# The last mixing chunk sent from SBUF to SBUF into the tokens, and tile 0's statistics moved ahead of the tables

## The chip, the cores and the metric

The kernel runs on one core of a Trainium2 chip. The metric is the device time of one execution in microseconds. Its median was 815.43 us in 3 runs (813.94 to 815.71).

## The reference, cut to what matters

The kernel computes one layer of a token-mixing tower. A state-space kernel of length 512 for 256 channels is generated from the input `x` (8, 256, 64, 2); its result is the token tensor `h` of 8 batches, 256 tokens (the channels of the mixing) and 512 features. To it come a windowed attention with rotary embedding on the layer norm of `h` (16 query heads, 4 key and value heads, head size 128, window 256) and a gated low-rank feed-forward on the layer norm of the sum.

```python
    # mixing: H, N, L = 256, 64, 512
    dtA = w * dt[:, None]
    Cm = Cc * (jnp.exp(dtA) - 1.0) / w
    h = 2 * jnp.einsum('chn,hnl->chl', Cm, jnp.exp(dtA[:, :, None] * jnp.arange(L))).real
    ...
    h = h + _L0_attn_ref(_layernorm(h, axis=-1), w_q, w_k, w_v, w_o)
    h = h + _L0_ffn_ref(_layernorm(h, axis=-1), ...)
```

Both matter here only through this: the layer norm of batch 0 needs the tokens of all 16 mixing chunks.

## The kernel before

**Mixing.** The 256 tokens are worked on in NQ = 16 chunks `q`. A chunk holds 8 tokens of each of two halves `hh` (tokens `hh*128 + 8q` to `hh*128 + 8q + 7`). For a chunk GpSimd, DVE and ACT write factor tables, TensorE multiplies 128 small pieces (`chunk`, L1426) into two PSUM banks, one for each `hh`, and counts `mixed`. ACT evacuates both banks into the stage tile `st[s]` (`evacuate`, L726) and counts `evac`. In `st` the partitions are (token parity t, batch c, feature block a) and the free dimensions four token pairs `m` and 64 features `j`.

**Through DRAM.** SP stores `st` into the DRAM tensor `mixed` (`store_mixed`, L427, two transfers of 128 KB, semaphore `xd_out[s]`) and loads tokens back into `x` (`load_tokens`, L431, two transfers of 64 tokens of one batch). `x` has 128 partitions, two token tiles t of 128 tokens, 8 batches and 512 features. Token tile 0 is made of the chunks 0 to 7, tile 1 of the chunks 8 to 15; partition `hh*64 + i` of tile t is token `hh*128 + 64t + i`. SP's order is written out by hand: after chunk 7 the load of tile 0 of batch 0 (`x_early`), then one store and one load in turn, then the store of chunk 15, a wait for all stores, and the loads of tile 1: batch 0 (`x_first`), batch 1 (`x_second`), batch 2 (`x_third`), two loads of weights, and the other batches (`x_rest`).

**The first layer norm, in halves.** DVE, after its last mixing work (L1054), multiplies the tables of the feed-forward (L1082 to L1085, twelve products, semaphore `pw_done`). Then it takes the statistics of tile 0 of batch 0 (`norm_stat`, L1089, and the aggregate at L1155, `early_var`), waits for GpSimd's `early_rstd`, applies the norm (`half_apply(0)`, L1145, `early_xn`), subtracts the rounded part of the transposed tile (`half_rest(0)`, L1149), waits for `x_first`, and does the same for tile 1 (aggregate L1164, `ln_var`, `half_apply(1)`). GpSimd waits for `pw_done`, makes the low part of the first weight chunk (`split_lo(0)`, L480), the reciprocal root for tile 0 (`early_norm`, L387, L540, L542), the low parts of the chunks 1 to 3 and then the root for tile 1 (`second_norm`, L387, L552, L554). ACT, after its last evacuation, copies `cw` (L761), loads the table of exponentials (L762) and copies the transposed halves (`xt_half`, L765). TensorE, after the last chunk, multiplies the tables (`cw_mm`, L1463), keeps its clock up with matmuls on constants (`keep_warm`, L1440), transposes tile 0 (L1473), keeps warm again, transposes tile 1 (L1473), keeps warm once more and begins the first projection (`split_product`, L1414 to L1416) with 48 matmuls of 256 columns.

**Order.** Every engine works its program in order, and a wait holds up all that stands behind it on that engine. The lines that set the order around the change are SP's list (L437 to L450), GpSimd's (L536 to L547), ACT's (L756 to L765), DVE's (L1076 to L1166) and TensorE's (L1461 to L1478).

Of the kernel before, what the change touches and what calls it, by code (L numbers as in the profile page):

```python
# [22 lines left out]
ACT = mybir.ActivationFunctionType  # L23
# [6 lines left out]
NS = 64  # L30
# [102 lines left out]
def tower(nc, mix_c, mix_s, log_dt, log_wr, w_im, w_qkv, w_o, w_gate, w_gmul, w_upd, centers, slopes, consts, out):  # L133
    x_dram = nc.dram_tensor("mixed", [S, NB, D], F32, kind="Internal").ap()
    top = ExitStack()
    with top:
        def sem(name):
            return top.enter_context(nc.semaphore(name))
# [171 lines left out]
        def raw_turn(n):  # L310
# [18 lines left out]
            sem("early_var"), sem("early_pool"), sem("early_rstd"), sem("early_xn"), sem("early_xt"), sem("early_hi"),  # L329
            sem("early_lo"), sem("x_early"))  # L330
        pw_done, cw_mm, cw_done = sem("pw_done"), sem("cw_mm"), sem("cw_done")
        ln_st, ln_var, ln_pool, ln_rstd, xn_ready = (
# [19 lines left out]
        def half_rows(hh):  # L352

            return slice(hh * NS, (hh + 1) * NS)

        def tokens_of(hh, t):

            first = hh * P + t * NS
            return slice(first, first + NS)
# [33 lines left out]
        def _(sp):  # L393
# [30 lines left out]
            def store_mixed(q, s, evacuated):  # L424
                sp.wait_ge(evac, evacuated)
                for hh in range(2):
                    sp.dma_start(rows[q, hh], st[s][:, hh, :, :]).then_inc(xd_out[s], 16)  # L427

            def load_tokens(t, b, done):
                for hh in range(2):  # L430
                    sp.dma_start(x[half_rows(hh), t, b, :], x_dram[tokens_of(hh, t), b, :]).then_inc(done, 16)  # L431

# [6 lines left out]
            for b, done in ((1, x_second), (2, x_third), (3, x_rest), (4, x_rest), (5, x_rest), (6, x_rest), (7, x_rest)):  # L439
                q = NQ // 2 + b - 1  # L440
                store_mixed(q, q % 2, q + 1)
                load_tokens(0, b, done)
            store_mixed(NQ - 1, 1, NQ)
            for s in range(2):
                sp.wait_ge(xd_out[s], 16 * 2 * (NQ // 2))
            load_tokens(1, 0, x_first)
            load_tokens(1, 1, x_second)
            load_tokens(1, 2, x_third)
# [22 lines left out]
        def _(pool):  # L471
# [57 lines left out]
            for hh in range(2):  # L529
                if hh:  # L530
                    pool.wait_ge(pb_done, 2)
                with pool.Fori(hh * NQ // 4 or 1, (hh + 1) * NQ // 4) as it:
                    for s in range(2):
                        pool.wait_ge(mixed, it * 2 + (s - 1))
                        chunk(it * 2 + s, s)
            pool.wait_ge(pw_done, KC)  # L536
            def early_norm():
# [5 lines left out]

            split_lo(0)
            early_norm()
            for n in range(1, KC):
                split_lo(n)  # L547
# [109 lines left out]
        def _(act):  # L657
# [86 lines left out]
            for lo, hi in ((1, TURN_AT), (TURN_AT, NQ // 2 - 1)):  # L744
                if lo == TURN_AT:
                    turn_p(1)
                with act.Fori(lo, hi) as it:
                    for s in range(2):
# [6 lines left out]
                        evacuate(it * 2 + s, s)  # L755
            for s in range(2):  # L756
                act.wait_ge(mixed, NQ - 1 + s)
                act.wait_ge(xd_out[s], (NQ // 2 - 1) * 32)
                evacuate(NQ - 2 + s, s)
            act.wait_ge(cw_mm, 1)  # L760
# [161 lines left out]
        def _(dve):  # L922
# [139 lines left out]
            for lo, hi in ((1, TURN_AT), (TURN_AT, NQ // 2)):  # L1062
# [6 lines left out]
                with dve.Fori(lo, hi) as it:  # L1069
                    for s in range(2):  # L1070
# [3 lines left out]
                        sum_b(s, it * 2 + s)  # L1074

            dve.wait_ge(gate_in, 80)  # L1076
            for k in range(KC):
# [8 lines left out]
                                dbs[:, k, :].unsqueeze(2).to_broadcast([P, NE, HE]), ALU.mult).then_inc(pw_done, 1)  # L1086

            def norm_stat(src, t):
                v.bn_stats(stats[:, t, :], src(t)).then_inc(ln_st, 1)  # L1089

# [25 lines left out]
            def tokens(b):  # L1116
                return lambda t: x[:, t, b, :]
# [33 lines left out]

            dve.wait_ge(x_early, 32)
            norm_stat(tokens(0), 0)
            wait_apart(dve, ln_st, 1, 4)
            v.bn_aggr(norm_set(0)["mv"][:, 0, :], stats[:, 0, :]).then_inc(early_var, 1)  # L1155
            dve.wait_ge(early_rstd, 1)
            half_apply(0).then_inc(early_xn, 1)
            for q in range(2):
                dve.wait_ge(early_hi, q + 1)
                half_rest(q, 0, 5 + q).then_inc(early_lo, 1)  # L1160
            dve.wait_ge(x_first, 32)
            norm_stat(tokens(0), 1)
            wait_apart(dve, ln_st, 2, 4)
# [243 lines left out]
        def _(pe):  # L1407
# [57 lines left out]

            pe.wait_ge(evac, NQ)
            keep_warm(2)

# [327 lines left out]
```

## Time and profile before

| | before |
|---|---|
| median of 3 runs | 815.43 us (813.94 to 815.71) |
| the profiled execution | 815.9 us |
| its span, first to last instruction | 813.8 us |
| TensorE busy | 748.4 us (92%) |
| VectorE (DVE) busy | 571.2 us (70%) |
| ScalarE (ACT) busy | 456.3 us (56%) |
| GpSimd (POOL) busy | 447.3 us (55%) |
| mean granted clock of TensorE | 0.994 |

The profile is of one execution. PE is TensorE, PEld its weight loads, SPq and ACTq the issue of transfers on SyncE and ScalarE. L with a number is a line of the kernel. The granted clock is given as a share of 2.4 GHz. The end of matmuls is modelled. A row of a timeline may merge several instructions of one line; its count stands behind the x. What ended the idle time before an instruction is inferred from semaphores and stands in brackets.

### The profile page before, as it was taken

How to read it: one execution, taken by the hardware profiler on the slowest of the kernel's cores; microseconds unless marked ns; L12 is line 12 of the kernel's file. 1: busy time of each engine (PE TensorE's matmuls, PEld its weight loads, DVE VectorE, ACT ScalarE, POOL GpSimd, SP SyncE). 2: the span in 40 equal slices, each digit the busy share in tenths (PEclk: the TensorE clock that was granted, in tenths of full speed). 3: DMA queues.
4: the chain of work that ended last, by engine and by line, in shares of the span. 5: the costliest groups of instructions: out<-in, count | busy, mean ns of one | idle time of the engine just before them, and what ended most of it. 6: DMA issues, size and time to landing. Idle time of an engine off the chain costs nothing.

```text
span 813.8 us, 19725 instructions
## 1 busy us (share of the span) xinstructions
PE 748.4 (92%) x6968; PEld 679.0 (83%) x6968; DVE 571.2 (70%) x1603; ACT 456.3 (56%) x1252; POOL 447.3 (55%) x663
## 2 busy tenths in 40 slices
PE   0377788999999999999999999999999999999996
PEld 0166667899999999999999999999999998988873
DVE  7989868877765655565665566666655777778876
ACT  6734436565567566555575655555756645545432
POOL 1488847655545646444465654444747565565532
PEclk9999999999999999999999999999999999999999
DMA  9023741100010102000001020000100001110104
GB/s 213 0 55 86 173 130 27 39 1 0 0 41 1 53 1 79 0 0 0 0 14 40 10 69 0 0 0 0 30 24 2 1 2 27 26 26 0 27 8 96
DMA packets 32215, 26.47 MB, mean 33 GB/s; under 512 B 23134, under 2 KB 23518, under 8 KB 32166
## 3 DMA queue, kind: packets, MB, share of 16 engines
q1 hardware_dynamic: 32022, 25.77, 12.7%
q8 instruction: 28, 0.46, 0.2%
q14 instruction: 21, 0.17, 0.1%
q10 hardware_dynamic: 144, 0.07, 0.0%
HBM read 17.44 MB, written 8.39 MB: 32 GB/s over the span
## 4 chain that ended last, share of the span: by engine, by line
PE 77%; POOL 7%; DVE 7%; ACT 4%; issue 3%; DMA 1%; DVEq 0%; SPq 0%; POOLq 0%; ACTq 0%
PE bank_quad L1414 17%; PE bank_quad L1416 16%; PE bank_quad L1415 16%; PE bank_pair L1414 4%; PE bank_pair L1416 4%; PE bank_pair L1415 4%; POOL w_lo L480 2%; PE bank_quad L1426 2%; PE bank_quad L1529 2%; PE bank L1607 1%; PE bank_pair L1597 1%; PE bank L1611 1%; PE bank_pair L1607 1%; DVE bank_pair L1043 1%; POOL kq_lo L572 1%
## 5 line engine op out<-in xcount | busy, mean ns | idle before, releaser
L1414 PE MATMUL bank_quad<-xt_hi,w_hi 128*128 (+1 forms) x768 | 216.7, 282 | 1.7 <-POOL w_lo L480 0.8
L1416 PE MATMUL bank_quad<-xt_lo,w_hi 128*128 (+1 forms) x768 | 214.4, 279 | 0.0
L1415 PE MATMUL bank_quad<-xt_hi,w_lo 128*128 (+1 forms) x768 | 214.3, 279 | 0.0
L1130 DVE TENSOR_TENSOR kq<-bank_quad,cst 128x512 f32<-128x512 f32 (+1 forms) x96 | 57.8, 603 | 134.3 <-ACT swap L793 101.2
L567 POOL TENSOR_TENSOR swap<-swap,cst 128x512 f32<-128x512 f32 (+1 forms) x96 | 106.0, 1106 | 81.2 <-ACT swap L793 77.0
L1414 PEld LDWEIGHTS bank_quad<-xt_hi,w_hi 128*128 128x128 f32 x768 | 144.2, 188 | 3.4 <-POOL w_lo L480 1.5
L1416 PEld LDWEIGHTS bank_quad<-xt_lo,w_hi 128*128 128x128 f32 x768 | 144.2, 188 | 0.0
L1415 PEld LDWEIGHTS bank_quad<-xt_hi,w_lo 128*128 128x128 f32 x768 | 143.9, 187 | 0.0
L387 POOL TENSOR_TENSOR spare<-cst 1x1 f32<-1x1 f32 x86 | 17.8, 208 | 200.3 <-DVE rinv L1296 139.7
L838 ACT ACTIVATE sm<-sm,mx 128x128 f32<-128x128 f32 (+1 forms) x256 | 113.6, 445 | 20.6 <-DVE mx L1284 20.6
L792 ACT ACTIVATE swap<-bank_quad 64x512 f32<-64x512 f32 (+1 forms) x96 | 50.3, 524 | 118.0 <-PE bank_quad L1416 115.1
L605 POOL TENSOR_SCALAR sm<-sm,rinv 128x128 f32<-128x128 f32 (+1 forms) x256 | 104.4, 421 | 0.9
L850 ACT ACTIVATE ot_hi<-bank_quad 128x512 fp32r<-128x512 f32 x64 | 37.8, 597 | 110.2 <-PE bank_quad L1416 110.2
L1136 DVE TENSOR_TENSOR kq<-kq,swap 128x512 f32<-128x512 f32 (+1 forms) x96 | 94.9, 1012 | 4.7 <-POOL swap L567 4.7
L572 POOL TENSOR_TENSOR kq_lo<-kq,kq_hi 128x256 fp32r<-128x256 f32 x93 | 78.5, 869 | 19.9 <-ACT kq_hi L804 19.9
L1275 DVE TENSOR_TENSOR ot_lo<-bank_quad,ot_hi 128x512 fp32r<-128x512 f32 x64 | 43.4, 677 | 25.7 <-ACT ot_hi L850 25.6
L1414 PE MATMUL bank_quad<-wo_hi,ot_hi 128*128 128x512 f32 x132 | 54.5, 413 | 0.4 <-DVE ot_lo L1275 0.4
L1416 PE MATMUL bank_quad<-wo_lo,ot_hi 128*128 128x512 f32 x132 | 51.9, 394 | 0.0
L1415 PE MATMUL bank_quad<-wo_hi,ot_lo 128*128 128x512 f32 x132 | 51.8, 393 | 0.0
L793 ACT ACTIVATE swap<-bank_quad 64x512 f32<-64x512 f32 (+1 forms) x96 | 49.9, 520 | 1.1
L1416 PE MATMUL bank_pair<-wo_lo,ot_hi 128*128 128x512 f32 x124 | 48.4, 390 | 0.0
L1415 PE MATMUL bank_pair<-wo_hi,ot_lo 128*128 128x512 f32 x124 | 48.2, 389 | 0.0
(332 smaller groups left out, 1867.7 us busy)
## 6 DMA issues: line engine op xcount, KB each, us to landing
mixed<-st SPq DMA_DIRECT2D x32, 128.0 KB, 2.0
x<-mixed SPq DMA_DIRECT2D x32, 128.0 KB, 3.1
out<-x SPq DMA_DIRECT2D x32, 128.0 KB, 2.3
raw<-in_w_qkv SPq DMA_DIRECT2D x8, 384.0 KB, 3.7
raw<-in_w_o SPq DMA_DIRECT2D x10, 256.0 KB, 2.7
norm_mem<-in_w_qkv SPq DMA_DIRECT2D x6, 384.0 KB, 3.7
norm_mem<-in_w_o SPq DMA_DIRECT2D x6, 256.0 KB, 2.8
cim<-in_mix_s SPq DMA_DIRECT2D x4, 256.0 KB, 7.9
```

The lines of the kernel that those rows point to most:

```text
L567: nc.gpsimd.tensor_tensor(view(sw), view(sw), table(sinT), ALU.mult).then_inc(rot_sin, 1)
L572: nc.gpsimd.tensor_tensor(flat(kl), part(kq), flat(kh).bitcast(F32), ALU.subtract).then_inc(kq_lo, 1)
L605: last = nc.gpsimd.tensor_scalar(sm[:, j, cols], sm[:, j, cols], rinv[:, 2 * j + t:2 * j + t + 1], 1.0, ALU.mult, ALU.mult)
L792: nc.scalar.activation(view(sw)[0:64], src[64:128], ACT.Copy)
L793: last = nc.scalar.activation(view(sw)[64:128], src[0:64], ACT.Copy)
L838: last = nc.scalar.activation(sm[:, j, cols], sm[:, j, cols], ACT.Exp, scale=-1.0, bias=mx[:, n:n + 1], accum_out=rsum[:, n:n + 1])
L1130: v.tensor_tensor(view(kq), src, table(cosT), ALU.mult).then_inc(kq_cos, 1)
L1136: v.tensor_tensor(view(kq), view(kq), view(sw), ALU.add).then_inc(kq_rot, 1)
L1275: v.tensor_tensor(by_rows(otl, j), natural(banks[j]), by_rows(oth, j).bitcast(F32), ALU.subtract).then_inc(ot_lo, 1)
L1414: mmul(dst, lh, rh, start=start and k == 0, stop=False, skip_group_check=True)
L1415: mmul(dst, ll, rh, start=False, stop=False, skip_group_check=True)
L1416: last = mmul(dst, lh, rl, start=False, stop=stop and k == n - 1, skip_group_check=True)
```

## The change

Chunk 15 no longer goes through DRAM. Its two banks are evacuated by two engines, bank 2 (`hh` = 0) by ACT and bank 3 (`hh` = 1) by DVE, each with a semaphore of its own. `last_rows` then sends each of the four token pairs `m` of a half straight from `st[1]` to two partitions of `x`, all batches at once: four transfers for `hh` = 0 issued by SP and four for `hh` = 1 issued by ACT, all counted on `x_last`. The loads of tile 1 shrink from 64 to 56 tokens. On SP the four stand behind the loads of batch 0, on ACT ahead of the copy of `cw`. DVE's statistics and aggregate of tile 0 move ahead of the table products. GpSimd makes the root for tile 0 first and all four low parts behind it, after `early_xn`. TensorE waits for chunk 14's evacuation instead of chunk 15's and keeps warm once instead of twice.

```diff
+        last_evac, x_last = [sem(f"last_evacuated{k}") for k in range(2)], sem("x_last_rows")
...
+        def last_rows(engine, hh):
+
+            first = hh * NS + NS - QH8
+            engine.wait_ge(last_evac[hh], 1)
+            for m in range(QH8 // 2):
+                engine_of = nc.sync if hh == 0 else nc.scalar
+                engine_of.dma_start(x[first + 2 * m:first + 2 * m + 2, TT - 1, :, :], st[1][:, hh, m, :]).then_inc(x_last, 16)
...
             def load_tokens(t, b, done):
+                n = NS if t == 0 else NS - QH8
                 for hh in range(2):
-                    sp.dma_start(x[half_rows(hh), t, b, :], x_dram[tokens_of(hh, t), b, :]).then_inc(done, 16)
+                    at, tok = half_rows(hh).start, tokens_of(hh, t).start
+                    sp.dma_start(x[at:at + n, t, b, :], x_dram[tok:tok + n, b, :]).then_inc(done, 16)
...
-            store_mixed(NQ - 1, 1, NQ)
             for s in range(2):
-                sp.wait_ge(xd_out[s], 16 * 2 * (NQ // 2))
+                sp.wait_ge(xd_out[s], 16 * 2 * (NQ // 2 - s))
             load_tokens(1, 0, x_first)
+            last_rows(sp, 0)
             load_tokens(1, 1, x_second)
...
-            pool.wait_ge(pw_done, KC)
             def early_norm():
...
-            split_lo(0)
             early_norm()
-            for n in range(1, KC):
+            pool.wait_ge(early_xn, 1)
+            pool.wait_ge(pw_done, KC)
+            for n in range(KC):
                 split_lo(n)
...
-            for s in range(2):
-                act.wait_ge(mixed, NQ - 1 + s)
-                act.wait_ge(xd_out[s], (NQ // 2 - 1) * 32)
-                evacuate(NQ - 2 + s, s)
+            act.wait_ge(mixed, NQ - 1)
+            act.wait_ge(xd_out[0], (NQ // 2 - 1) * 32)
+            evacuate(NQ - 2, 0)
+            act.wait_ge(mixed, NQ)
+            act.wait_ge(xd_out[1], (NQ // 2 - 1) * 32)
+            nc.scalar.activation(st[1][:, 0, :, :].rearrange("p m j -> p (m j)"), banks[2][:, 0:4 * 64],
+                                 ACT.Copy).then_inc(last_evac[0], 1)
+            last_rows(act, 1)
...
+            dve.wait_ge(x_early, 32)
+            norm_stat(lambda t: x[:, t, 0, :], 0)
+            wait_apart(dve, ln_st, 1, 4)
+            v.bn_aggr(norm_set(0)["mv"][:, 0, :], stats[:, 0, :]).then_inc(early_var, 1)
+
             dve.wait_ge(gate_in, 80)
...
-            dve.wait_ge(x_early, 32)
-            norm_stat(tokens(0), 0)
-            wait_apart(dve, ln_st, 1, 4)
-            v.bn_aggr(norm_set(0)["mv"][:, 0, :], stats[:, 0, :]).then_inc(early_var, 1)
             dve.wait_ge(early_rstd, 1)
             half_apply(0).then_inc(early_xn, 1)
+            dve.wait_ge(mixed, NQ)
+            dve.wait_ge(xd_out[1], (NQ // 2 - 1) * 32)
+            v.tensor_copy(st[1][:, 1, :, :].rearrange("p m j -> p (m j)"), banks[3][:, 0:4 * 64]).then_inc(last_evac[1], 1)
             for q in range(2):
                 dve.wait_ge(early_hi, q + 1)
                 half_rest(q, 0, 5 + q).then_inc(early_lo, 1)
             dve.wait_ge(x_first, 32)
+            dve.wait_ge(x_last, 16 * 8)
             norm_stat(tokens(0), 1)
...
-            pe.wait_ge(evac, NQ)
-            keep_warm(2)
+            pe.wait_ge(evac, NQ - 1)
+            keep_warm(1)
```

## Rows read from the trace of the kernel before

**Rows 1.** The page, the chain that ended last, shares of the span by engine.

```profile
PE 77%; POOL 7%; DVE 7%; ACT 4%; issue 3%; DMA 1%; DVEq 0%; SPq 0%; POOLq 0%; ACTq 0%
```

**Rows 2.** The chain in order of time, 95 to 110: start us, us, what.

```profile
98.27 0.67 ACT st L726 x2
...
99.37 2.16 DMA mixed<-st
...
102.14 2.92 DMA x<-mixed
105.09 0.70 DVE stats L1089
...
107.25 0.56 DVE norm_mem L1145
```

**Rows 3.** Timeline of GpSimd: start us, us, engine, line, operation [idle before, releaser].

```profile
97.21 1.82 POOL L480 TENSOR_TENSOR w_lo<-raw,w_hi 128x768 fp32r<-128x768 f32 x1 [2.27 <-DVE vtab L1085]
...
100.05 1.80 POOL L480 TENSOR_TENSOR w_lo<-raw,w_hi 128x768 fp32r<-128x768 f32 x1
101.81 3.79 POOL L480 TENSOR_TENSOR w_lo<-raw_more,w_hi 128x768 fp32r<-128x768 f32 x2
106.13 0.18 POOL L387 TENSOR_TENSOR spare<-cst 1x1 f32<-1x1 f32 x1 [0.53 <-DVE norm L1164]
```

**Rows 4.** Timeline of DVE, 95 to 104.

```profile
95.65 0.22 DVE L1082 TENSOR_TENSOR vtab<-fw 128x64 f32<-128x64 f32 x1
...
97.03 0.71 DVE L1089 BATCH_NORM_STATS2 stats<-x 128x6 f32<-128x512 f32 x1
...
100.12 2.02 DVE L1145 TENSOR_SCALAR norm_mem<-x,norm 128x512 f32<-128x512 f32 x1 [2.12 <-POOL norm L542]
103.08 0.42 DVE L1149 TENSOR_TENSOR xt_lo<-bank_pair,xt_hi 128x256 fp32r<-128x256 f32 x1 [0.95 <-ACT xt_hi L765]
```

**Rows 5.** Timelines of SP's issues and of ACT, 95 to 101.

```profile
95.79 0.93 SPq L427 DMA_DIRECT2D mixed<-st  x2
96.76 1.20 SPq L431 DMA_DIRECT2D x<-mixed  x2
...
99.67 1.28 ACT L762 ACT_TABLE_LOAD   x1
```

**Rows 6.** Issues and chain at the start; windows (engines busy, PEclk, DMA share, GB/s).

```profile
0.74 0.72 SPq L394 DMA_DIRECT2D lg<-in_log_dt  x1
...
0.73 0.39 ACTq L665 DMA_DIRECT2D lg<-in_log_wr  x1
...
0.74 3.54 DMA lg<-in_log_dt
...
2.20:2.40 0.20, 0.00 (x0) 0.00 (x0) 0.00 (x0) 0.20 (x1) 0.00 (x0) 1.00 0.14 44
5.50:6.00 0.50, 0.00 (x0) 0.00 (x0) 0.47 (x2) 0.00 (x0) 0.00 (x0) 1.00 1.06 408
50.50:51.50 1.00, 0.06 (x5) 0.06 (x6) 1.00 (x2) 0.00 (x0) 0.94 (x1) 1.00 1.05 218
```

**Rows 7.** Timeline of TensorE, 99 to 108.

```profile
99.16 1.88 PE L1440 MATMUL bank_quad<-cst 128*128 128x512 f32 x4
102.19 0.44 PE L1473 MATMUL bank_pair<-cst,norm_mem 128*128 128x128 f32 x2 [1.15 <-DVE norm_mem L1145]
...
102.68 3.60 PE L1440 MATMUL bank_quad<-cst 128*128 128x512 f32 x8
107.94 0.41 PE L1473 MATMUL bank<-cst,norm_mem 128*128 128x128 f32 x2 [1.67 <-DVE norm_mem L1145]
```

**Rows 8.** TensorE after two idle stretches, and the window behind the second.

```profile
34.02 7.46 PE L1440 MATMUL bank_quad<-cst 128*128 128x512 f32 x10 [34.02 <-DVE vtab L1004]
...
66.11 0.38 PE L1435 MATMUL bank_quad<-bt,g 64*128 64x2 f32 x2 [2.92 <-DVE bt L1054]
...
66.00:72.00 6.00, 5.89 (x252) 5.75 (x256) 5.50 (x7) 2.04 (x8) 3.34 (x3) 0.72 0.17 35
```

More of the change, by code:

```diff
@@ L1074, in _, with norm_stat @@
                         sum_b(s, it * 2 + s)
+            def norm_stat(src, t):
+                v.bn_stats(stats[:, t, :], src(t)).then_inc(ln_st, 1)
+            dve.wait_ge(x_early, 32)
+            norm_stat(lambda t: x[:, t, 0, :], 0)
+            wait_apart(dve, ln_st, 1, 4)
+            v.bn_aggr(norm_set(0)["mv"][:, 0, :], stats[:, 0, :]).then_inc(early_var, 1)
             dve.wait_ge(gate_in, 80)
@@ L1086, in _ @@
                                 dbs[:, k, :].unsqueeze(2).to_broadcast([P, NE, HE]), ALU.mult).then_inc(pw_done, 1)
-            def norm_stat(src, t):
-                v.bn_stats(stats[:, t, :], src(t)).then_inc(ln_st, 1)
             def norm_collect(m):
```

## The prediction, made before the changed kernel ran

> **What bounds the kernel now.** I read three views in this order: the chain that ended last, then each engine's timeline around the hand-over from mixing to the layers, then the windows. Over the whole span the chain is mostly TensorE [rows 1], so from about 150 us on anything that starts TensorE later makes the end later by the same amount. The change touches only 95 to 110 us, where the chain is one transfer after another. Mixing's last chunk ends in ACT's evacuation at 98.27 us; SP issues its store in two halves, the second from 99.37, which lands in DRAM at 101.53 (99.37 + 2.16), the load back lands at 105.06 (102.14 + 2.92), and only then can DVE take tile 1's statistics at 105.09 [rows 2]. From 98.27 to 105.09 are 6.8 us, which is what the change aims at.
>
> Behind that chain stands a second one that is nearly as late. GpSimd splits four weight chunks (L480): it waits for the tables until 97.21, stops for tile 0's norm, and ends at 105.60 (101.81 + 3.79). It then waits 0.53 us for DVE's aggregate and starts tile 1's norm at 106.13, whose end releases `half_apply(1)` at 107.25 [rows 2, 3]. The time to be won is therefore not 6.8 us but what GpSimd leaves.
>
> **Tile 0's statistics ahead of the tables.** DVE's table products start at 95.65 [rows 4] and end at 97.03, where the statistics start [rows 4]. Exchanged, the statistics start at 95.65. For tile 1 it is 1.04 us from their start (105.09) to GpSimd's norm (106.13), and 1.12 us more to the apply (107.25) [rows 2, 3]. GpSimd is idle at this place (2.27 us before its first split [rows 3]), so it starts at 96.7 and `early_rstd` comes at 97.8. The tables end at 98.0. `half_apply(0)` then runs with GpSimd idle: 0.56 us as at 107.25 [rows 2], not 2.02 beside a running split [rows 4]. `early_xn` comes at about 98.6, 3.5 us before 102.14. GpSimd's four splits now wait for it and run without a stop: 98.63 + 1.80 for the first + 5.55 for the other three (100.05 to 105.60) = 105.98 [rows 3]. Tile 1's norm can thus start at 105.98, against 106.13. The greatest gain of the whole change is 0.15 us, whatever the transfers do.
>
> **The evacuation in two halves.** ACT copies bank 2 (98.27 to 98.65), DVE copies bank 3 after `half_apply(0)`. The copy of 256 columns from PSUM is bounded by 0.42 us, DVE's 256-column read of PSUM beside a running split [rows 4], and by 2.02 us if it had to wait as the apply did. I take 0.42, because the row of 0.42 also reads PSUM; DVE is done at 99.05.
>
> **The order of SP's queue.** The store of chunk 15 goes. SP is free at 97.96, after the loads that start at 96.76 [rows 5]. Chunk 14's store lands at about 98.35, since its second half is issued some 0.5 us behind 95.79 and takes the 2.1 us of a store [rows 2, 5]. The two loads for `x_first` are then issued from 98.4 to 99.6 (1.20 a pair [rows 5]), and behind them the four row transfers. The loads of the next batches come behind these. Issued at about 102.6 as they were before at 102.8, they cost nothing, as long as tile 1 is later than they are.
>
> **The eight row transfers: where the time goes.** Each writes 8192 floats into two partitions from 128 partitions, that is 128 pieces of 256 B. The trace has no SBUF-to-SBUF transfer. It has one that is two entries wide at its outermost level: the load of `log_dt`, whose source is two rows. Its issue took 0.72 us, ACT's ordinary one of the same bytes 0.39, and it landed 3.54 us after its issue; while it ran alone the DMA share was 0.14 at 44 GB/s, 2.2 of 16 engines at 20 GB/s each [rows 6]. A 512-B packet thus took 512 B / 20 GB/s, 25 ns. So a transfer with two entries outermost on one side ran on two engines, and the eight new ones have two partitions outermost on their destination side. I take two engines, and the same two for all eight, as SP's and ACT's transfers share the 16 engines.
>
> The Trainium skill, "DMA: Bandwidth & Descriptors", section "Why a DMA increments its semaphore by 16 and not by 1", says that the number of engines is the largest up to 16 that divides the slowest dimension of both sides, and that they are always the lowest-numbered ones. By that rule a two-partition destination gets two engines; for a source side the `log_dt` row agrees, for a destination side no row shows it.
>
> How long does a 256-B packet take an engine? Stores of such packets ran at 218 GB/s on all 16, 13.6 GB/s each: 256 / 13.6 = 18.8 ns, say 19. From below it is bounded by the trace's highest rate, 408 GB/s, 25.5 each: 10 ns. From above by the 25 ns of the `log_dt` packets [rows 6]. I take 19, since that row has the same packet size and an SBUF source. Per engine: 8 x 64 = 512 packets x 19 = 9.7 us. ACT's first is issued at 99.05, and ends issuing at 99.77. Around the data lie 0.9 us: chunk 15's store took 2.16 us from the end of its first issue (99.37) to its landing [rows 2], and its 262 KB at 218 GB/s are 1.2 of these. I put two thirds of it before the data (an estimate; only the sum matters): data from 100.4. SP's own begin by 101. `x_last` is complete at 100.4 + 9.7 + 0.3, plus 0.2 for the `x_first` packets ahead: 110.6. Tile 1's statistics start there and not at 105.09 [rows 2]: **+5.5 us**. With 10 ns it is +0.9, with 25 ns +8.6.
>
> ACT issues its four ahead of `cw`, 4 x 0.72 = 2.9 us from 99.05. Queued behind are the copy of `cw`, the table load of 1.28 us [rows 5] and tile 0's two `xt_hi` halves; these come at about 103.7 against 102.66, DVE's `half_rest(0)` at 104.1 to 104.9 against 103.08 [rows 4]. All that lies under the wait for `x_last`; were the transfers quick, 104.9 would still be under GpSimd's 105.98, less 1.0 us of statistics.
>
> **TensorE's clock.** Before, TensorE keeps warm for 1.88 us from 99.16, transposes tile 0 at 102.19, keeps warm for 3.60 from 102.68 to 106.28, idles 1.67 us and starts tile 1 at 107.94 [rows 7]. Now it has one `keep_warm` fewer (0.94 us), transposes at about 100.1 and is done at 100.1 + 0.5 + 3.6 = 104.2. Tile 1's transposes come at 107.94 + 5.5 = 113.4: 9 us idle. The trace shows what shorter idling did: 2.92 us before 66.11, and within 66 to 72 us the granted clock averaged 0.72, which is 6 x 0.28 / 0.5 = 3.4 us at the lower level of 1.2 GHz [rows 8]. After the 34 us idle at the start, ten records took 7.46 us, where eight take 3.60 when warm (0.45 each) [rows 7, 8]: 3.0 us lost, 5.9 us at the lower level. Behind tile 1's transposes stand a `keep_warm` and 48 projection matmuls with ACT waiting for them, so the lost time is on the path, at least 3.4 / 2 = 1.7 and at most 3.0: I take **+2.4 us**.
>
> **The sum.** The profiled execution took 815.9 us with a span of 813.8, the rest lies around it; the median of the runs, 815.43, is 0.5 lower. 815.9 + 5.5 + 2.4 = 823.8 on the profile's scale, and 815.43 + 7.9 = 823.3 on the median's, which I give. Nothing takes it back: the early batches are a chain, and after that TensorE is the bound.
>
> **Rivals.**
> 1. Two engines, but packets at the rate of the trace's fastest stretch, 10 to 12 ns (chance 0.15). `x_last` is complete at 106.0 to 107.1, +0.9 to +2.0, and TensorE still idles about 5 us, +1.7 to +3.0: 818.0 to 820.4. Against it stands the only 256-B row from SBUF [rows 6]; for it, that this row ends in DRAM and the new transfers do not. The Trainium skill, same page, section "Why small descriptors are slow (HBM only)", says that SBUF-to-SBUF transfers don't suffer from small descriptors, and speaks for this rival and against my 19 ns. No row shows such a transfer.
> 2. The destination's shape does not matter and all 16 engines share it (0.20). 1024 packets over 16 engines are 1.2 us, so issue bounds it: SP's last is issued by 102.5, landed by 104.5, and GpSimd decides. That is -0.15 and 815.3 if the clock holds (0.08); TensorE idles 3.6 us from 104.2 to 107.8, longer than the 2.92 that went before a slow stretch, and then it is 817.0 to 818.3 (0.12). For it: only the source side is seen in the trace.
> 3. Faster by over 0.2%, the other side (0.03). The place is GpSimd, with all engines sharing the transfers: if its four splits ran quicker now that nothing interrupts them, tile 1's norm would start when DVE lets it, which with issues of 0.39 us instead of 0.72 is at 104.4: -1.7 us, 813.7. It decides only where the splits together fall below 5.9 us, from 7.35; the two on `raw` took 1.82 and 1.80 [rows 3], with DVE's apply beside the second and not beside the first, so nothing supports it.
> My forecast has the remaining 0.62.
>
> **How the numbers follow.** The forecast's own range is 821 to 827 (clock 1.7 to 3.0, packets 17 to 25 ns). The range for 8 in 10 leaves out the held clock (0.08), the gain (0.03) and some of the top: 816.8 to 827.0. About 0.2%, 1.6 us, is what measurement can tell from no change, and the bound is 817.1. Slower: 0.62 + 0.15 and half of the clock's loss in rival 2, 0.83. Same: 0.14. Faster: 0.03.
>
> **What would show it.** Right: DVE's statistics of tile 1 (now L1089 at 105.09) wait for a DMA `x<-st` until about 110.6; the DMA share between 102 and 110 is near 0.13 wherever no loads run; issues of L431's neighbours take 0.7 us each; GpSimd sits idle from 106 to 111; the granted clock falls to 0.5 around 108 to 117. `early_xn` near 98.6 shows the statistics' move right. Wrong: an `x<-st` landing within 2.5 us of its issue means all engines share it; a landing at 106 to 107, the quick packets; GpSimd's norm started by its own last split at 106.0, rival 2.

## The result, and the profile after

The changed kernel took 826.24 us (median of 6 runs, 822.71 to 827.55) where the kernel before took 815.57 us in the same comparison (6 runs, 813.94 to 816.29). The ratio is 1.0127, with a 95% interval of 1.0106 to 1.0148: slower by 10.7 us. The forecast was 823.3 us, 7.9 us above the median before.

| | before | after |
|---|---|---|
| span of the profiled execution | 813.8 us | 824.7 us |
| tile 1's statistics of batch 0 start | 105.09 | 115.13 |
| batch 3's statistics start | 137.20 | 148.52 |
| TensorE busy | 748.4 us | 747.9 us |
| mean granted clock of TensorE | 0.994 | 0.986 |

The spans differ by 10.9 us, and the table says where they come from. Tile 1's statistics start 10.04 us later. From there to batch 3's statistics the kernel before takes 137.20 - 105.09 = 32.11 us, and the one after 148.52 - 115.13 = 33.39 us: another 1.28. From there to the end it is 676.6 us before and 676.2 us after. Batch 2's statistics, at 125.69 against 114.35, are already 11.34 us late, so all of the loss arises between 98 and 126 us.

The chain that ended last, in order of time around the hand-over (start us, us, what), of after:

```profile
96.61 1.34 POOL spare L396
...
98.29 0.57 POOL norm L552
...
102.35 12.69 DMA x<-st
...
115.13 0.71 DVE stats L1092
...
117.29 0.56 DVE norm_mem L1165
...
117.98 0.66 PE bank L1493 x2
```

Where the store and the load back stood, 2.16 and 2.92 us [rows 2], there is now one row transfer of 12.69 us. Its issue is the last of ACT's four, from 102.35 to 104.98, and stands inside the 12.69. These are timelines of after: SP's issues and ACT, from 96 us.

```profile
96.68 2.58 SPq L442 DMA_DIRECT2D x<-mixed  x4
99.31 3.82 SPq L363 DMA_DIRECT2D x<-st  x4
103.17 2.69 SPq L442 DMA_DIRECT2D x<-mixed  x4
105.91 0.96 SPq L416 DMA_DIRECT2D raw<-in_w_o  x2
```

```profile
98.20 0.38 ACT L772 ACTIVATE st<-bank_quad 128x256 f32<-128x256 f32 x1 [2.51 <-PE bank_quad L1446]
...
99.80 5.18 ACTq L363 DMA_DIRECT2D x<-st  x4
105.03 0.28 ACT L776 ACTIVATE cw<-bank 128x136 f32<-128x136 f32 x1 [6.45 <-issue]
```

ACT's four issues take 5.18 us, 1.3 each, not 0.72. From 103.17 on SP issues the loads of the other batches, while ACT's rows are still on their way. DVE and GpSimd of after, in the same stretch:

```profile
95.57 0.70 DVE L1092 BATCH_NORM_STATS2 stats<-x 128x6 f32<-128x512 f32 x1
...
98.89 0.55 DVE L1165 TENSOR_SCALAR norm_mem<-x,norm 128x512 f32<-128x512 f32 x1 [0.99 <-POOL norm L552]
99.35 0.42 DVE L1176 COPY st<-bank_quad 128x256 f32<-128x256 f32 x1
107.13 0.42 DVE L1169 TENSOR_TENSOR xt_lo<-bank_pair,xt_hi 128x256 fp32r<-128x256 f32 x1 [7.36 <-ACT xt_hi L780]
...
115.13 0.69 DVE L1092 BATCH_NORM_STATS2 stats<-x 128x6 f32<-128x512 f32 x1 [7.25 <-DMA x<-st]
```

```profile
96.61 1.34 POOL L396 TENSOR_TENSOR spare<-cst 1x1 f32<-1x1 f32 x1 [1.75 <-DVE norm L1097]
...
103.04 3.62 POOL L491 TENSOR_TENSOR w_lo<-raw_more,w_hi 128x768 fp32r<-128x768 f32 x2
116.17 0.18 POOL L396 TENSOR_TENSOR spare<-cst 1x1 f32<-1x1 f32 x1 [9.51 <-DVE norm L1184]
```

DVE waits 7.25 us for `x<-st`, and GpSimd has been idle for 9.51 us when it starts tile 1's norm. Its last split is done at 106.66 (103.04 + 3.62). The windows of after (PE, PEld, DVE, ACT, POOL busy, then the granted clock, the DMA share and GB/s) show how the transfers ran:

```profile
101.00:105.00 4.00, 2.98 (x7) 0.96 (x6) 0.00 (x0) 0.00 (x0) 4.00 (x4) 1.00 0.18 37
108.00:115.00 7.00, 0.00 (x0) 0.00 (x0) 0.00 (x0) 0.00 (x0) 0.00 (x0) 0.51 0.77 218
115.00:122.00 7.00, 4.02 (x14) 2.97 (x15) 3.81 (x11) 0.77 (x2) 1.31 (x5) 0.51 0.03 10
```

While rows run nearly alone the share is 0.18, that is 2.9 of 16 engines at 37 GB/s, where 16 engines moved packets of the same size at 218 GB/s [rows 6]. From 108 to 115 no compute engine does anything, the loads hold the DMA share at 0.77, and TensorE's clock is at its lower level of 1.2 GHz.

What became of ACT's rows in that time stands in the DMA view of after, by queue (packets, MB, share of 16 engines), first for 105 to 107, then for 109 to 111. q1 is SP's queue, q10 ACT's:

```profile
q1 hardware_dynamic: 259, 0.33, 59.0%
q10 hardware_dynamic: 197, 0.05, 11.7%
...
q1 hardware_dynamic: 299, 0.49, 89.7%
q10 hardware_dynamic: 46, 0.01, 3.1%
```

ACT's rows go at 98 packets per us while the loads begin and at 23 once they run in full. That their last packets wait among the loads' packets of 2 KB is inferred from these rates; e1 tests it.

### The profile page after: what moved, and what is told of

It reads as the page before. It is cut to its first block, busy times and chain, and to the rows that moved or that the text cites. A ratio compares the mean times of both kernels' runs of the same rounds, so it can differ in the third digit from the quotient of the medians.

```text
span 824.7 us, 19729 instructions
## 1 busy us (share of the span) xinstructions
PE 747.9 (91%) x6966; PEld 679.1 (82%) x6966; DVE 569.8 (69%) x1604; ACT 455.5 (55%) x1251; POOL 447.2 (54%) x663
## 4 chain that ended last, share of the span: by engine, by line
PE 75%; DVE 8%; POOL 7%; ACT 3%; issue 3%; DMA 2%; ACTq 0%; DVEq 0%; POOLq 0%
PE bank_quad L1434 16%; PE bank_quad L1436 16%; PE bank_quad L1435 16%; PE bank_pair L1436 4%; PE bank_pair L1434 4%; PE bank_pair L1435 4%; POOL w_lo L491 2%; PE bank_quad L1549 2%; DMA x<-st 2%; PE bank L1627 1%; PE bank_pair L1617 1%; PE bank L1631 1%; PE bank_pair L1627 1%; PE bank_quad L1446 1%; DVE bank_pair L1058 1%
## 5 line engine op out<-in xcount | busy, mean ns | idle before, releaser
L1434 PE MATMUL bank_pair<-wo_hi,ot_hi 128*128 128x512 f32 x124 | 48.2, 389 | 0.0
```

Source lines behind the costliest of these rows:

```text
L1434: mmul(dst, lh, rh, start=start and k == 0, stop=False, skip_group_check=True)
```

## The experiments

Line numbers in the rows are those of each kernel. Theory A, the account that the first runs test: the rows share two DMA engines because their destinations are two partitions each; alone they would be complete at about 109; the rest of the delay comes from the loads that SP issues behind its own rows and that meet ACT's on the same engines; the clock costs about 1.3 us more. Its rivals: the packets of the rows are slow in themselves, whatever else runs (then e1 moves little), or it is the small packets and not their destination (then e2 moves little). Each kernel was compared with the kernel before on the same chip: its median was 816.53 us beside e1 to e4, 815.59 beside e5, e6, e8 and e9, and 816.63 beside e10. The differences given are to these. Edits are shown against the changed kernel where nothing else is said.

**e1. The loads behind all rows.** SP waits for every row before it issues the loads of batch 1 and on.

```diff
             last_rows(sp, 0)
+            sp.wait_ge(x_last, 16 * 8)
             load_tokens(1, 1, x_second)
```

> The changed kernel, but SyncE waits for all eight row transfers before it issues the loads of batch 1 and later and the two weight loads. In the changed kernel the rows' 256-B packets leave two engines at 135 a microsecond from 101 to 105 us, and once the loads are in flight ScalarE's rows get only 6 to 35 a microsecond. Theory A (two engines, and the loads that share them delay ScalarE's rows): undisturbed, 1024 packets at 135 a microsecond take 7.6 us, x_last is complete at 108.5 to 109.5 instead of 115.0, the loads are issued from there in time, and the kernel takes 826.2 - 6 = 820.5, between 819.5 and 821.5. Theory B (the rows are slow by themselves, the packets of two queues into one pair of partitions hinder each other): x_last stays at 114 to 116 and the kernel is at 826 or later.

Measured: 822.58 us, ratio 1.0073 (1.0052 to 1.0094), +6.0 us; span 820.3. Chain, DVE's timeline and window of this kernel:

```profile
102.73 6.86 DMA x<-st
```

```profile
109.68 0.69 DVE L1093 BATCH_NORM_STATS2 stats<-x 128x6 f32<-128x512 f32 x1 [1.54 <-DMA x<-st]
```

```profile
101.00:105.00 4.00, 3.25 (x8) 1.14 (x6) 0.00 (x0) 0.00 (x0) 4.00 (x3) 1.00 0.17 35
```

```profile
DMA packets 505, 0.14 MB, mean 35 GB/s; under 512 B 498, under 2 KB 498, under 8 KB 505
```

The row transfer at the end takes 6.86 us instead of 12.69, and the statistics start at 109.68. Mixing ended 0.27 us later in this execution than in after (ACT's evacuation at 98.47 against 98.20), so on after's scale it is 109.4, 5.7 us before 115.13. That is the loads' part, shown by moving them and nothing else. Its size rests on one execution of each kernel: in e3, which leaves all transfers as they are, the statistics start 0.95 us earlier than in after on the same scale (113.75, mixing ended at 97.77), and the medians, +10.7 and +6.0 us, differ by 4.6. So it is 5.7 give or take about 1 us. The rows landed at 109.59 (102.73 + 6.86) and the kernel is at +6.0, both just beyond what was expected (108.5 to 109.5; 819.5 to 821.5, which is +3.9 to +5.9 over the 815.57 of that comparison). The last line counts the packets of 101 to 105: 505 in 4 us are 126 per us. If two engines carry them, one packet of 256 B takes 2 / 126 = 15.8 ns, and all 1024 take 8.1 us.

From the apply of tile 1 to batch 3's statistics this kernel still needs 1.58 us more than before (31.53 against 29.95), most likely the clock: TensorE idles here too, and the granted clock is 0.50 from 108 to 115.

**e2. The same packets on all engines.** The rows are sent to the stage tile `st[0]`, with its 128 partitions as destination, in pieces of 256 B as before. Both issuers also wait until chunk 14 has left `st[0]`; SP's first issue stands at 99.69 against 99.31, ACT's at 99.86 against 99.80. Left out is that chunk 15's tokens reach `x`: tile 1 is loaded as 64 tokens from 8 further up.

```diff
+            engine.wait_ge(xd_out[0], 16 * NQ)
             for m in range(QH8 // 2):
-                engine_of.dma_start(x[first + 2 * m:first + 2 * m + 2, TT - 1, :, :], st[1][:, hh, m, :]).then_inc(x_last, 16)
+                engine_of.dma_start(st[0][:, hh, m, :], st[1][:, hh, m, :]).then_inc(x_last, 16)
...
-                n = NS if t == 0 else NS - QH8
+                n = NS
...
-                    at, tok = half_rows(hh).start, tokens_of(hh, t).start
+                    at, tok = half_rows(hh).start, tokens_of(hh, t).start - (QH8 if t else 0)
```

> The changed kernel, but each of the eight transfers writes its 128 packets of 256 B to 128 partitions of the free stage tile instead of to two partitions of x. The tokens of the last chunk therefore do not reach x, and the loads of tile 1 take the 64 tokens from 8 further up. Same bytes, same packets, same queues. Theory A (the two-partition destination puts a transfer on two engines): the DMA share during the rows is no longer 0.15, each lands within 2.5 us of its issue, all by 105, tile 1's norm is started by GpSimd at 106.7 and the kernel takes 816 to 817.7, its excess over before being the norm's 0.5 us and what the clock loses. Theory B (SBUF to SBUF is slow in itself, or the two queues are): landing as late as in the changed kernel, 824 or more.

Measured: 818.14 us, ratio 1.0017 (1.0007 to 1.0027), +1.6 us; span 814.9. After's window of 101 to 103 comes first; then this kernel's windows, the packets of 101 to 103, a row of its chain, and ACT's issues:

```profile
101.00:103.00 2.00, 2.00 (x6) 0.80 (x6) 0.00 (x0) 0.00 (x0) 2.00 (x2) 1.00 0.15 32
```

```profile
101.00:103.00 2.00, 2.00 (x6) 0.83 (x5) 0.00 (x0) 0.47 (x2) 2.00 (x2) 1.00 0.57 128
...
108.00:110.00 2.00, 1.48 (x5) 1.25 (x6) 0.74 (x2) 0.74 (x2) 0.00 (x0) 0.50 0.89 271
```

```profile
DMA packets 1005, 0.26 MB, mean 128 GB/s; under 512 B 989, under 2 KB 989, under 8 KB 1005
```

```profile
107.83 0.56 DVE norm_mem L1166
```

```profile
99.86 2.60 ACTq L364 DMA_DIRECT2D st<-st  x4
```

The share of the same two microseconds is 0.57 instead of 0.15, 989 small packets go in them, a row transfer lands 2.1 us after its issue, ACT's four issues take 2.60 us instead of 5.18, and the statistics start at 105.29. The packets, their size and their source are the same, only the destination is another: two partitions instead of 128 kept the rows on few engines. And yet the kernel is not faster: GpSimd is done with its splits at 106.7 and then decides; tile 1's apply comes at 107.83 against 107.25 [rows 2], +0.58, and the clock stands at 0.50 from 108 to 110, +0.79 by the way from the apply to batch 3's statistics (30.74 against 29.95). Together 1.37. This is the forecast's rival 2 in what it does, and in size its lower end: 817.0 to 818.3 is +1.6 to +2.9 over the 815.43 from which it was counted. So even with all engines the change would not be faster.

**e3. The clock held up.** TensorE works on constants until tile 1 comes.

```diff
-            keep_warm(4)
+            keep_warm(17)
```

> The changed kernel with 17 instead of 4 matmuls on constants behind tile 0's transposes, which keeps TensorE busy until about 115.7 us. Theory: the granted clock no longer falls (it was at 0.5 from 108.4 to 121.8), x_last stays at 115, and what the lower clock cost is given back, 9.69 against 8.39 us from the start of half_apply(1) to ScalarE's second swap copy: 1.3 us, 824.9. My prediction had put 2.4 us on it, which would give 823.8. Rival: the clock costs nothing since the other engines are waited for, 826.2.

Measured: 824.81 us, ratio 1.0110 (1.0068 to 1.0151), +8.3 us; span 822.7. Window of this kernel over the same 14 us:

```profile
108.00:122.00 14.00, 11.85 (x53) 7.02 (x52) 4.63 (x13) 1.18 (x4) 2.01 (x6) 1.00 0.34 108
```

The granted clock stays at 1.00 and the stretch from the apply (115.90) to batch 3's statistics (145.85) is 29.95 us, to the hundredth that of before. After's is 31.23. The clock's cost is 1.28 us, shown. The time itself hits the expected 824.9 by luck: the kernel before took 1.0 us more beside this run, and +8.3 is 2.4 less than after's +10.7. Besides the clock, the rows were complete earlier in the profiled execution, by the 0.95 us named under e1.

**e4. The statistics alone.** The kernel before, with DVE's and GpSimd's part of the change (statistics ahead of the tables, as in the diff of the change, and the four splits behind `early_xn`) and without the row transfers. GpSimd's edit, against the kernel before:

```diff
-            pool.wait_ge(pw_done, KC)
...
-            split_lo(0)
             early_norm()
-            for n in range(1, KC):
+            pool.wait_ge(early_xn, 1)
+            pool.wait_ge(pw_done, KC)
+            for n in range(KC):
                 split_lo(n)
```

> The kernel before with only tile 0's statistics ahead of the tables and GpSimd's four splits behind early_xn; chunk 15 goes through DRAM as before. By my prediction GpSimd ends its splits at 106.0 and the kernel is at -0.15 us, 815.4. By the trace after, GpSimd's one-element operation at 96.61 took 1.34 us beside DVE's table products, early_xn came at 99.4 and the splits ended at 106.7: then tile 1's norm starts 0.5 us later than before and the kernel takes 816.1. Rival: the earlier statistics gain the 2 us by which tile 0 is ahead, 813.5.

Measured: 817.52 us, ratio 1.0011 (1.0001 to 1.0022), +1.0; span 814.7. GpSimd's timeline, and then the chain:

```profile
96.96 1.33 POOL L387 TENSOR_TENSOR spare<-cst 1x1 f32<-1x1 f32 x1 [1.75 <-DVE norm L1082]
```

```profile
98.63 0.57 POOL norm L541
...
99.23 0.56 DVE norm_mem L1150
...
99.85 7.15 POOL w_lo L480 x4
107.00 0.15 POOL spare L387
```

The four splits are now on the chain, end at 107.00, and tile 1's norm starts right behind. Of the possible gain of 0.15 us nothing is there: tile 1's apply comes at 108.08 against 107.25, 0.56 later when mixing's own 0.27 us of delay in this execution is taken off. The one-element operation that opens GpSimd's norm took 1.33 us and ended where DVE's table products end; elsewhere it takes 0.18 [rows 3].

**e9. The tables behind the apply.** The kernel of e4, with the table products behind `half_apply(0)`, so that nothing of DVE's runs beside GpSimd's norm.

```diff
-            dve.wait_ge(gate_in, 80)
-            for k in range(KC):
...
             half_apply(0).then_inc(early_xn, 1)
+            dve.wait_ge(gate_in, 80)
+            for k in range(KC):
...
```

> The kernel with the statistics alone moved, and DVE's twelve table products behind half_apply(0). It asks why GpSimd's one-element operation took 1.34 us instead of 0.18. Theory A (a GpSimd operation that reads SBUF waits while DVE runs operations with two inputs in SBUF): with DVE idle at this place it takes 0.2 us, early_xn comes 1.1 us earlier than with the tables in front, at about 98.7, and the splits start at 100.2 behind the tables. Theory B (GpSimd needs a while to start after standing idle): it takes 1.3 us again.

Measured: 816.72 us, ratio 1.0020 (1.0010 to 1.0030), +1.1; span 814.3. GpSimd's timeline and DVE's:

```profile
96.60 0.18 POOL L387 TENSOR_TENSOR spare<-cst 1x1 f32<-1x1 f32 x1 [1.75 <-DVE norm L1082]
```

```profile
97.72 0.55 DVE L1139 TENSOR_SCALAR norm_mem<-x,norm 128x512 f32<-128x512 f32 x1 [1.20 <-POOL norm L541]
```

The operation takes 0.18 us again, and the apply comes 1.5 us earlier (97.72 against 99.23), 1.2 when the 0.35 us by which mixing ended earlier is taken off. So it was DVE's products that held it up. As a whole it wins nothing, since the splits wait for the tables (99.79) and end as late as in e4 (106.97).

**e5. The rows alone.** The row transfers without the moved statistics. DVE's half of the evacuation stands behind `half_apply(0)`, which here runs late.

```diff
+            pool.wait_ge(pw_done, KC)
...
+            split_lo(0)
             early_norm()
-            pool.wait_ge(early_xn, 1)
-            pool.wait_ge(pw_done, KC)
-            for n in range(KC):
+            for n in range(1, KC):
                 split_lo(n)
```

> Only the other part of the change: chunk 15 goes from SBUF to SBUF, but tile 0's statistics stay behind the tables and GpSimd's first split ahead of tile 0's norm, as before. DVE comes to bank 3 only behind half_apply(0), which runs beside a split until 102.1, so ScalarE's four are issued from 102.6, 2.8 us later than in the changed kernel. If the loads behind them decide, x_last is complete at 116 to 119 and the kernel is 11 to 14 us slower than before. If the part that moves the statistics were what costs the time, this kernel would be as fast as the one before.

Measured: 832.35 us, ratio 1.0213 (1.0195 to 1.0231), +16.8 us; span 830.3. The chain, ACT's issues and DVE's timeline:

```profile
108.05 12.22 DMA x<-st
```

```profile
102.86 7.76 ACTq L363 DMA_DIRECT2D x<-st  x4
```

```profile
120.37 0.69 DVE L1092 BATCH_NORM_STATS2 stats<-x 128x6 f32<-128x512 f32 x1 [6.84 <-DMA x<-st]
```

ACT's rows start 3.06 us later than in after (102.86 against 99.80) and the statistics start 5.24 us later (120.37 against 115.13), 2.6 and 4.8 when the 0.45 us by which mixing ended later is taken off: more of the rows meet the loads, and ACT's issues take 7.76 us. So within the change the moved statistics help the rows by about 5 us (5.6 us of span, 830.3 - 824.7, less the 0.45), since they let DVE evacuate its bank early; without rows to help they win nothing. The size was missed, 16.8 where 11 to 14 were expected.

**e6. All rows on SP.** All eight rows stand ahead of the loads of the next batches, in one queue.

```diff
-                engine_of = nc.sync if hh == 0 else nc.scalar
+                engine_of = nc.sync
...
             last_rows(sp, 0)
+            last_rows(sp, 1)
...
-            last_rows(act, 1)
```

> The changed kernel with all eight row transfers issued by SyncE, ahead of the loads of batch 1 and later; ScalarE issues none. The same 1024 packets on the same two engines, but in one queue in which the loads stand behind them. Theory A (what delayed the rows to 115 us are the loads, taken in turn with ScalarE's queue): x_last is complete at about 108.5 to 110, as when SyncE waited for it, and the kernel is 5.5 to 7 us slower than before. Theory B (two issuers were a help, a queue alone is slower): x_last at 114 or later, 10 us or more slower than before.

Measured: 825.61 us, ratio 1.0129 (1.0114 to 1.0145), +10.0; span 823.6; statistics at 113.47. Its window of 101 to 105 with the packets in it:

```profile
101.00:105.00 4.00, 2.82 (x7) 0.95 (x5) 0.76 (x2) 0.47 (x2) 4.00 (x4) 1.00 0.17 21
```

```profile
DMA packets 339, 0.09 MB, mean 21 GB/s; under 512 B 339, under 2 KB 339, under 8 KB 339
```

The 109 of theory A was missed, and +10.0 is what theory B gave. The share is the same 0.17, but only 339 packets went in 4 us, 85 per us and 23.6 ns for one on two engines, half as much again as the 15.8 with two queues. So either one queue is slower than two, or rows to the same few partitions follow each other more slowly than rows to both halves in turn. In e5 SP's four went alone in the same way from 102 to 105, at 81 per us (242 packets in 3 us). Not all of the delay is the packets: the loads, issued from 107.93, move in the same queue while the last row transfer, landed at 113.37, is still under way (0.22 MB from 110 to 111).

**e10. The halves in turn on SP.** Again one queue, but each `m` sends its `hh` = 0 and its `hh` = 1 one after the other.

```diff
             for m in range(QH8 // 2):
-                engine_of.dma_start(x[first + 2 * m:first + 2 * m + 2, TT - 1, :, :], st[1][:, hh, m, :]).then_inc(x_last, 16)
+                for hh in range(2):
+                    first = hh * NS + NS - QH8
+                    nc.sync.dma_start(x[first + 2 * m:first + 2 * m + 2, TT - 1, :, :], st[1][:, hh, m, :]).then_inc(x_last, 16)
```

> All eight row transfers on SyncE, ahead of the loads, but the two halves in turn (partitions 56 and 57, then 120 and 121, and so on) instead of four of one half and then four of the other. With one queue the packets left at 66 to 110 a microsecond, with two queues at 116 to 140. Theory A (one queue on an engine hides less of each packet's latency, whatever it writes): the rate stays at 66 to 110 and x_last is complete at 112 to 114. Theory B (packets of one transfer into one partition hinder each other, and two queues were faster only since they wrote to two regions): the turns do not help inside a transfer, but where two transfers overlap; a rate of about 130 and x_last at 108 to 110 would show it.

Measured: 823.76 us, ratio 1.0090 (1.0061 to 1.0119), +7.1; span 821.5. The same lines of this kernel, and DVE's timeline:

```profile
101.00:105.00 4.00, 2.83 (x7) 0.95 (x5) 0.76 (x2) 0.48 (x2) 4.00 (x4) 1.00 0.17 34
```

```profile
DMA packets 500, 0.13 MB, mean 34 GB/s; under 512 B 499, under 2 KB 499, under 8 KB 499
```

```profile
111.00 0.69 DVE L1093 BATCH_NORM_STATS2 stats<-x 128x6 f32<-128x512 f32 x1 [9.01 <-DMA x<-st]
```

With 500 packets in the 4 us the rate of two queues is back with one queue, which speaks for the destinations and against the number of queues. But it does not last. From 101 to 102 there go 144 packets, from 105 to 106 only 63, at about the same share (0.16 and 0.18), and over 101 to 109 it is 922, 115 per us, between e6's 90 (722) and e1's 131 (1050). The rows are complete only at 111.0, between the two theories' times. Nothing in the trace says why the rate falls. What sets the time of one packet stays open, and two executions of this kernel are few.

**e8. A smaller way.** The kernel before, with the store of chunk 15 kept, but batch 0's first 56 rows of each half loaded already behind chunk 14's store, so that only 8 rows of each half are loaded behind chunk 15's; and GpSimd's fourth split behind tile 1's apply.

```diff
-            for s in range(2):
-                sp.wait_ge(xd_out[s], 16 * 2 * (NQ // 2))
-            load_tokens(1, 0, x_first)
+            def load_part(lo, hi, done):
+                for hh in range(2):
+                    at, tok = half_rows(hh).start, tokens_of(hh, 1).start
+                    sp.dma_start(x[at + lo:at + hi, 1, 0, :], x_dram[tok + lo:tok + hi, 0, :]).then_inc(done, 16)
+            sp.wait_ge(xd_out[0], 16 * 2 * (NQ // 2))
+            load_part(0, NS - QH8, x_first)
+            sp.wait_ge(xd_out[1], 16 * 2 * (NQ // 2))
+            load_part(NS - QH8, NS, x_last)
...
-            for n in range(1, KC):
+            for n in range(1, KC - 1):
                 split_lo(n)
...
+            pool.wait_ge(xn_ready, 1)
+            split_lo(KC - 1)
```

> A candidate on the kernel before, chunk 15 through DRAM: batch 0's 56 rows of tile 1 are loaded while chunk 15's store is under way, and only its 8 last rows of each half behind the store; GpSimd's fourth split comes behind half_apply(1). The load that ends the chain took 2.92 us for 128 KB; with 16 KB I expect 2.0, so statistics at 104.2 instead of 105.1, apply at 106.4, and the fourth split, 1.8 us from 107.0 to 108.8, ready when the first projection starts at 108.9. Expected 0.9 us faster than before, at the edge of what can be measured; 0 if the small load takes as long as the large one, and 1 us slower if the projection waits for the split.

Measured: 814.59 us (11 runs), ratio 0.9990 (0.9981 to 0.9999), -1.0 us; span 812.2. The chain of this kernel:

```profile
100.37 2.03 DVE norm_mem L1153
...
103.33 0.49 DVE xt_lo L1157 x2
...
104.01 0.69 DVE stats L1097
```

Tile 1's statistics start at 104.01 and their releaser is DVE's own `half_rest(0)`, no longer a transfer, and with GpSimd's fourth split out of the way the apply comes at 106.15 against 107.25. It beats both kernels, but by 0.1% over the one before: the interval leaves out 1, barely, and the gain is below the 0.2% that I said can be told from no change. The transfer is out of the chain here, and that was worth about 1 us of the 6.8.

## Why the prediction was right or wrong

**What bounds it: right.** The gain was to be capped by GpSimd, and a loss in front of batch 0's tile 1 was to reach the end. Both held: with the rows on all engines (statistics at 105.29) the kernel still lost, and of the 11.3 us that after loses up to batch 3 (10.04 + 1.28) 10.9 are in its span.

**Few engines for a two-partition destination: right.** The forecast took it from `log_dt`, a source two entries wide [rows 6]. For the destination side e2 shows it, 0.57 of the DMA engines against 0.18. That they are exactly two is not shown: no view lists the engines, and a share of 0.17 to 0.18 is 2.7 to 2.9 of them, of which I can't account for the part above two. The share is no strict count either: two windows of [rows 6] have 1.05 and 1.06 of all 16. By the Trainium skill, "DMA: Bandwidth & Descriptors", section "Why a DMA increments its semaphore by 16 and not by 1", it would be two, the largest number up to 16 that divides the slowest dimensions of both sides, 128 and 2; the trace agrees that there are few and that the destination decides.

**The packets: a little too dear.** 19 ns was the term, from stores to DRAM; 15.8 were measured in e1. Alone, the rows cost 109.4 - 105.09 = 4.3 us instead of 5.5. Rival 1's 10 to 12 ns was not seen. The Trainium skill, same page, section "Why small descriptors are slow (HBM only)", would have SBUF to SBUF unharmed by small pieces. The measured 15.8 to 23.6 ns stand beside 18.8 for stores of such packets [rows 6], and e2's share gives 18 ns with 128 partitions too (0.57 x 16 engines x 2 us / 1005 packets, an estimate), so these runs don't bear it out.

**"They cost nothing": wrong, and this is the step that failed.** The forecast set the loads of the next batches behind SP's four rows and took them for free as long as tile 1 was later than they are. They stand behind SP's rows, but ACT's four are in another queue, and their last issue ends at 104.98 (99.80 + 5.18) while the loads are issued from 103.17. The loads take 0.90 of all 16 engines (109 to 111), so also most of those on which ACT's rows wait, and in packets eight times as large. The rows were complete about 5.7 us later for it. Of the 10.04 us in front of the statistics that is more than half, and it was priced at nothing. The same argument in the forecast, that SP's and ACT's transfers share the engines, was applied to the rows and not to the loads.

**ACT's issues: mis-sized.** 5.18 us instead of 2.9, and 2.60 when the same packets went to all engines: so the issues were held by where the rows went. The 0.72 was one transfer's, alone at the start. `cw` came at 105.03 instead of 102, `half_rest(0)` at 107.13 instead of 104.1; all of it lay under the wait, as said.

**The clock: right in kind, too large in size.** It fell to the lower level as said, from about 108 until 121.8, and cost 1.28 us instead of 2.4. TensorE was at the lower level for over 13 us, but for the first 10 of these, up to 117.98, it had nothing to do. Its work there, 3.9 us from 117.98 to 121.84, is what cost time. The chain shows the same projection matmul before and after:

```profile
110.66 0.12 PE bank_quad L1414
```

```profile
122.00 0.12 PE bank_quad L1434
```

Counted from tile 1's apply, that is 3.41 us before (110.66 - 107.25) and 4.71 after (122.00 - 117.29). The 1.30 between them is the whole cost; 1.28 is left of it at batch 3. The forecast's lower end, 1.7, was nearer than its middle, which took a part of the 34 us idle at the start as its measure; this place does not resemble that one.

**The statistics: half right.** They started at 95.57 as forecast (95.65), but `early_xn` came at 99.44 (98.89 + 0.55) and not at 98.6, as GpSimd's first operation took 1.34 us and not 0.18. The apply itself, with GpSimd idle, took 0.55 as said. In the changed kernel it cost nothing, since the rows were later. In e4 the splits, held back by it, made tile 1 0.56 us later. DVE's copy of the second bank took 0.42 us, as said.

**The sum.** Terms: rows 5.5 forecast, 4.3 measured; loads 0, 5.7; clock 2.4, 1.28. Measured 11.3 against 7.9 forecast; the two terms that were too dear, by 1.2 and 1.1 us, hid part of the 5.7 that was missing. The time, 826.24, lies within the range, near its upper end, and that is in part luck: with the rows and the clock sized as measured and the loads at nothing, the same sum gives +5.6 us, half of what came.

## What to carry to other kernels

Before a transfer is sent to a few partitions, count the partitions on its destination side as well as its bytes: here 1024 packets of 256 B to two partitions each needed about 8 us, where to 128 partitions 989 small packets went in two (e2). Then look at every queue that issues at the same time, also the one beside, because the order in one queue does not protect the transfers of the other from it (in e6 not even its own: loads moved behind rows that had not landed). And before a wait is shortened, read which chain is second: here, of 6.8 us of transfers, the best run (e8) got 1 us.

## What the hardware showed that was not expected

- Issuing can be held: four issues on ACT took 5.18 us with two-partition destinations, 2.60 with 128 partitions, and 7.76 in e5, where more of them met the loads. An engine that issues transfers and has other work behind them pays for it.
- A one-element operation of GpSimd took 1.34 us instead of 0.18 while DVE ran a row of table products back to back, each with two operands in SBUF, and 0.18 once they were moved away. The Trainium skill, "SBUF — State Buffer", section "Who interferes with whom", says that a DVE instruction with two SBUF inputs contends with a GpSimd instruction that reads SBUF; e4 and e9 agree, and show that it waited over several products, not one.
- Packets of 256 B from SBUF to two partitions took 15.8 ns (2 / 126, if two engines) from two queues, 16.0 from one queue with the halves in turn (500 packets in 4 us), and 23.6 from one queue with one half behind the other. These are means of 4 us; with the halves in turn it was 17.4 over 8 us (922 packets). Why is open.
- GpSimd's four splits without a stop took 7.15 to 7.18 us in e2, e4 and e9, whatever DVE did beside them.
